# First tile turned beside the weights, two places for rows of x, for queries and for the projection's tile, bias rows fetched one block later, scatter counted in batches

## The chip, the cores and the metric

The kernel runs on one core of one Trainium2 chip. The metric is the device time of one execution in microseconds (us). Beside it there is one profiled execution, from which every row below comes; its span goes from the first to the last instruction.

## What is computed

A graph transformer layer over N = 3125 nodes with D = 1024 features and 50000 edges. In short:

```python
xn = layernorm(x)
# graph attention, 4 heads of 256: softmax over the edges (src, dst) and one loop per node
xp = xn @ W;  e = leaky_relu(a_src[src] + a_dst[dst]);  alpha = softmax of e over each dst
gnn = relu(segment_sum(xp[src] * alpha, dst) + bias)
# linear attention, 16 heads of 64
Q = elu(xn @ Wq.T + bq) + 1;  K = elu(xn @ Wk.T + bk) + 1;  V = xn @ Wv.T + bv
KV = sum over nodes of K x V;  Z = Q . K.sum(0)
mix = ((Q @ KV) / (Z + 1e-6)) @ Wo.T + bo
x = x + gnn + mix
x = x + ffn(layernorm(x))     # 1024 -> 512 -> 1024, piecewise linear gelu, fixed point
```

## The kernel before

Nodes are handled in NT = 25 tiles of T = 125. A float32 product is made of three products of fp32r parts: `high` (ScalarE) writes the rounded part of an operand and `low` (VectorE) what is left of it, and `product` runs 3 x 8 matmuls of 512 columns for each half of 1024 columns; `project` does both halves, 48 matmuls. The program is a row of blocks. In each block every engine has its own list of instructions, with semaphores between them, and the next block begins when all engines have ended this one. The names used below:

- **weights of K and V** (first block of `keys_and_values`): `SplitWeights` loads 16 blocks of 128 rows into a ring of five (`raw`), TensorE turns each into one of two PSUM places, ScalarE and VectorE split it. VectorE normalises x's first tile here. Each edge's key (src * N + dst) is stored to `edge_keys`. At its end SyncE loads the bias rows `bk_row` and `bv_row`, which lie in the places of `raw`, spread over 125 partitions, and waits for them.
- **stage K** (second block): for each tile TensorE makes keys and values, turns the next tile (`turn_rows`), and sums K x V. VectorE runs `normalise` of the next tile, the bias sums, `Edges.prepare` and the sums. ScalarE `take`s the turned tile: copies it to `xT_whole`, writes its high part, and then loads `E_row`, the next 1000 edge keys spread over 125 partitions (`Edges.load`). SyncE loads x's rows and stores `xT_whole` to `xnT`. GpSimd zeroes the count matrix (50 transfers from `zeros`, each of 128 rows of 1527 words, four in flight) and then adds edges to it: `Edges.scatter` works off units of 1000 edges, each of two batches of four indirect DMAs, and every batch waits until the batch before has landed.
- **block P** (first block of `linear_attention`): the weights of the queries and the mixing matrix, and at its end the bias rows `bq_row` and `bo_row`.
- **stage Q** (second block): for each tile the projection `query`, its elu and scaling on VectorE, `turn_rows` of the scaled queries, and the projection `mix`; `finish` adds the result to x. `Edges.prepare` goes on for units 25 to 49, with `E_row` now loaded by SyncE.
- **stage V** (`graph_values`): 2 x 25 products of 24 matmuls over the tiles, first the left then the right half of the columns. In the second half, VectorE also runs 25 passes of `Nearest.step` over rows of counts, which SyncE may load when all edges are scattered.
- after them `graph_attention` and `feed_forward`, which the change does not touch.

GpSimd's share of the edges is fixed per stage: 20 units in K, 2 in P, 23 in Q and the last 5 in V. No scheduler is at work; the order on each engine is the order of the code.

Of the kernel before, what the change touches and what calls it, by code (L numbers as in the profile page):

```python
# [31 lines left out]
UNITS_K, UNITS_P, UNITS_Q = 20, 2, 23  # L32
# [5 lines left out]
ZW, ZN = 1527, 50  # L38
# [36 lines left out]
def gps_layer(nc, x, src, dst, gnn_w, att_src, att_dst, gnn_bias, wq, bq, wk, bk, wv, bv, wo, bo,  # L75
# [4 lines left out]
    counts_fill = counts.rearrange("(k p w) -> k p w", k=ZN, p=128)  # L80
# [177 lines left out]
class Edges:  # L258
# [57 lines left out]
    def scatter_unit(self, pool, counts_cells, u, slot):  # L316
# [9 lines left out]
        for c in range(CPU):  # L326
            if c and c % BATCH == 0:
                pool.wait_ge(self.scattered, u * (16 * CPU) + 16 * c)
                pool.sem_inc(self.seen, 1)
# [4 lines left out]
    def scatter(self, pool, counts_cells, first, until):  # L334
        if first == 0:
            self.scatter_unit(pool, counts_cells, 0, 0)
            first = 1
        pairs = (until - first) // 2
        with pool.Fori(0, pairs) as i:
            for k in range(2):  # L340
                self.scatter_unit(pool, counts_cells, i * 2 + (first + k), (first + k) % 2)
        if first + 2 * pairs < until:
            self.scatter_unit(pool, counts_cells, until - 1, (until - 1) % 2)
# [55 lines left out]
def keys_and_values(nc, st, a):  # L399
# [6 lines left out]
    zeros = sb("zeros", [128, ZW])  # L406

    rows = sb("rows", [T, D])
# [3 lines left out]
    x_loaded, xn_ready, stats_seen, first_link = sem("x_loaded"), sem("xn_ready"), sem("stats_seen"), sem("first_link")  # L412


    with ExitStack() as pst:
# [9 lines left out]
        rows_loaded = psem("rows_loaded")  # L425
# [3 lines left out]
        with nc.Block() as block:  # L429
            @block.sync  # L430
            def _(sp):
                for tile, e in ((src_c, a["src"]), (dst_c, a["dst"])):
                    sp.dma_start(tile[:, :, :], e.rearrange("(b c p) -> c b p", b=CB, p=CH)).then_inc(edges_loaded, 16)
                load_rows(sp, rows, a["x"][0:T, :], x_loaded)
# [28 lines left out]
            @block.scalar  # L463
            def _(act):
                weights.take_high(act, blocks)
                act.wait_ge(zeros_set, 1)

            @block.vector
            def _(dve):
                nc.vector.memset(zeros[:, :], 0.0).then_inc(zeros_set, 1)  # L470
# [4 lines left out]
                dve.wait_ge(x_loaded, 32)  # L475
                normalise(nc, chain, rows[:, :], rows[:, :], stats, moments, root, stats_seen).then_inc(xn_ready, 1)
                dve.wait_ge(keys_turned, 1)
                nc.vector.tensor_copy(edges.keys[:, :].rearrange("p (b c) -> p b c", b=CB), ktr[0:CH, :, 0:CR]).then_inc(keys_copied, 1)
                weights.take_low(dve, blocks)
# [1193 lines left out]
```

## Time and profile before

| | |
|---|---|
| median of 3 runs | 3458.6 us (3450.61 to 3459.63) |
| the profiled execution's own time | 3460.86 us |
| its span | 3459.1 us |
| TensorE busy | 3192.6 us (92%) |
| VectorE busy | 2705.0 us (78%) |
| GpSimd busy | 1015.0 us (29%), all but its last small transfers before 1510 us |
| mean granted TensorE clock | 0.972 of full speed |

The stages in the profiled execution, by the first instructions of each block: weights of K and V to 51.4 us, K to 721.4, P to 775.7, Q to 1383.1, V to about 1705. A row of the timeline gives the start in us, the duration in us, the engine, the line, what is done, and in brackets the idle time of that engine just before it and what ended it. "SPq" and "ACTq" are DMA issues; such a row's duration is that of the issue alone.

### The profile page before, as it was taken

How to read it: one execution, taken by the hardware profiler on the slowest of the kernel's cores; microseconds unless marked ns; L12 is line 12 of the kernel's file. 1: busy time of each engine (PE TensorE's matmuls, PEld its weight loads, DVE VectorE, ACT ScalarE, POOL GpSimd, SP SyncE). 2: the span in 40 equal slices, each digit the busy share in tenths (PEclk: the TensorE clock that was granted, in tenths of full speed). 3: DMA queues.
4: the chain of work that ended last, by engine and by line, in shares of the span. 5: the costliest groups of instructions: out<-in, count | busy, mean ns of one | idle time of the engine just before them, and what ended most of it. 6: DMA issues, size and time to landing. Idle time of an engine off the chain costs nothing. (4 is left out here: it accounts for less than half of the span.)

```text
span 3459.1 us, 43729 instructions
## 1 busy us (share of the span) xinstructions
PE 3192.6 (92%) x14812; PEld 2595.8 (75%) x14812; DVE 2705.0 (78%) x4736; ACT 1129.0 (33%) x1445; POOL 1015.0 (29%) x698
## 2 busy tenths in 40 slices
PE   6899999978999998998689999998999996899998
PEld 5678888857888886776568888887788885677776
DVE  5577777757777776558699999998999875788886
ACT  2011111121111111123245555555555443445444
POOL 1256777757767667720000000000000000000000
PEclk8999999999999999999899999999999998999999
DMA  7943333343444444445588878887788765222221
GB/s 260 363 81 66 54 70 55 61 125 75 95 86 91 85 95 114 94 107 154 151 211 222 228 214 219 218 218 213 213 220 218 185 165 151 69 89 71 71 89 42
DMA packets 332845, 484.90 MB, mean 140 GB/s; under 512 B 199146, under 2 KB 199246, under 8 KB 332726
## 3 DMA queue, kind: packets, MB, share of 16 engines
q1 hardware_dynamic: 142644, 401.03, 40.8%
q0 software_dynamic: 184656, 65.68, 11.0%
q10 hardware_dynamic: 5426, 16.70, 1.3%
q8 instruction: 64, 1.05, 0.1%
q14 instruction: 55, 0.45, 0.0%
HBM read 391.39 MB, written 90.80 MB: 139 GB/s over the span
## 5 line engine op out<-in xcount | busy, mean ns | idle before, releaser
L1357 PE MATMUL G_acc<-values,whole_plain 125*125 125x257 f32 x5000 | 1117.5, 385 | 82.6 <-DVE whole_plain L1317 67.4
L1357 PEld LDWEIGHTS G_acc<-values,whole_plain 125*125 125x125 f32 x5000 | 944.0, 190 | 246.2 <-DVE whole_plain L1317 80.1
L330 POOL DMA_INDIRECT counts<-E_twins_now,E_cells_now x400 | 874.3, 2186 | 378.5 <-issue 247.6
L1252 ACT ACTIVATE whole_plain<-whole_plain,G_asrc_slope 125x750 f32<-125x750 f32 (+1 forms) x400 | 375.9, 944 | 335.0 <-DVE whole_plain L1308 333.2
L1308 DVE SCALAR_TENSOR_TENSOR whole_plain<-whole_plain,G_asrc_most 125x750 f32<-125x750 f32 (+1 forms) x400 | 412.3, 1031 | 59.0 <-PE G_acc L1357 42.3
L1317 DVE SCALAR_TENSOR_TENSOR whole_plain<-whole_plain 125x750 f32<-125x750 f32 (+1 forms) x400 | 388.4, 971 | 49.6 <-ACT whole_plain L1252 49.5
L952 DVE SCALAR_TENSOR_TENSOR N_least<-xT_plain,asrc_all,N_least 125x750 f32<-125x750 bf16 (+1 forms) x336 | 340.3, 1018 | 0.0
L1226 POOL DMA_DIRECT2D gat<-xT_plain x100 | 53.4, 535 | 972.4 <-ACT xT_plain L1268 972.4
L227 PE MATMUL V_v_ps<-whole,xT_space 128*125 128x512 f32 x1200 | 293.3, 402 | 35.2 <-DVE xT_space L255 24.1
L227 PEld LDWEIGHTS V_v_ps<-whole,xT_space 128*125 128x125 f32 x1200 | 221.3, 187 | 106.9 <-DVE xT_space L255 42.5
L227 PE MATMUL Q_q_ps<-whole,xT_space 128*125 128x512 f32 x1200 | 288.2, 399 | 13.9 <-DVE xT_space L255 13.9
L227 PE MATMUL K_v_ps<-K_wv,xT_space 128*125 128x512 f32 x1200 | 293.7, 401 | 0.0
L227 PE MATMUL K_k_ps<-whole,xT_space 128*125 128x512 f32 x1200 | 288.3, 399 | 3.4 <-DVE xT_space L255 3.4
L227 PE MATMUL Q_mix_ps<-Q_mixer,xT_space 128*125 128x512 f32 x1200 | 282.0, 393 | 2.8 <-DVE xT_space L255 2.8
L227 PEld LDWEIGHTS Q_q_ps<-whole,xT_space 128*125 128x125 f32 x1200 | 222.7, 187 | 70.0 <-DVE xT_space L255 14.7
L302 DVE SCALAR_TENSOR_TENSOR E_scratch<-E_row,E_col,E_mask 125x500 bf16<-125x500 f32 x400 | 268.3, 736 | 2.3 <-DVE E_col L294 0.3
L227 PEld LDWEIGHTS K_k_ps<-whole,xT_space 128*125 128x125 f32 x1200 | 222.3, 187 | 60.5 <-DVE xT_space L255 3.8
L251 ACT ACTIVATE xT_space<-xT_whole 128x1000 fp32r<-128x1000 f32 x100 | 104.1, 1041 | 499.7 <-PE Q_q_ps L227 251.4
L227 PEld LDWEIGHTS Q_mix_ps<-Q_mixer,xT_space 128*125 128x125 f32 x1200 | 222.2, 185 | 58.6 <-DVE xT_space L255 3.1
L227 PEld LDWEIGHTS K_v_ps<-K_wv,xT_space 128*125 128x125 f32 x1200 | 224.6, 189 | 55.2
L936 ACT ACTIVATE xT_plain<-whole_plain,N_huge 125x750 bf16<-125x750 f32 (+1 forms) x175 | 164.1, 938 | 268.0 <-DMA whole_plain<-counts 224.5
L551 ACT ACTIVATE K_raw<-K_raw 125x1024 f32<-125x1024 f32 x25 | 26.5, 1059 | 571.3 <-DVE K_raw L578 571.3
(173 smaller groups left out, 3384.1 us busy)
## 6 DMA issues: line engine op xcount, KB each, us to landing
whole_plain<-counts SPq DMA_DIRECT2D x450, 328.1 KB
whole_plain<-counts SPq DMA_DIRECT2D x150, 382.8 KB
counts<-K_zeros POOLq DMA_DIRECT2D x50, 763.5 KB, 9.0
xT_whole<-xnT SPq DMA_DIRECT2D x75, 500.0 KB, 3.6
whole_plain<-counts SPq DMA_DIRECT2D x450, 38.1 KB
xnT<-xT_whole SPq DMA_DIRECT2D x25, 500.0 KB, 7.9
gat<-xT_plain POOLq DMA_DIRECT2D x100, 125.0 KB, 4.1
E_row<-edge_keys ACTq DMA_DIRECT2D x25, 488.3 KB
```

Source lines behind the costliest of these rows:

```text
L227: last = nc.tensor.matmul(out, stationary(s, b), moving(m, b), start=(n == 0), stop=(n == len(terms) - 1))
L251: return nc.scalar.activation(out, source, ACT.Copy)
L302: chain.step(nc.vector.scalar_tensor_tensor(out=self.scratch[:, c % 2, :], in0=batch, scalar=self.col[:, c:c + 1], in1=mask, op0=ALU.is_equal,
L330: nc.gpsimd.indirect_dma_start(out=counts_cells, out_offset=bass.IndirectOffsetOnAxis(ap=self.cells_now[:, slot, c:c + 1], axis=0), in_=se ...
L551: nc.scalar.activation(ex[:, :], ex[:, :], ACT.Exp).then_inc(k_exp, 1)
L936: self.nc.scalar.activation(absent[:, n % 2, 0:w], ring[:, slot, 0:w], ACT.Relu, bias=self.huge[:, :], scale=-ABSENT).then_inc(self.absent ...
L952: self.nc.vector.scalar_tensor_tensor(out=here, in0=mask, scalar=term, in1=here, op0=ALU.subtract, op1=ALU.min).then_inc(self.least_ready, 1)
L1226: pool.dma_start(a["gat_dram"][(at + t) * T:(at + t + 1) * T, h * C:(h + 1) * C], sums[:, t, 0:C]).then_inc(gat_stored, 16)
L1252: nc.scalar.activation(here, here, ACT.Exp, bias=asrc_slope[:, u % H, j:j + 1]).then_inc(exp_ready, 1)
L1308: nc.vector.scalar_tensor_tensor(out=weight[:, k % RING, 0:w], in0=rows[:, u % 2, 0, 0:w], scalar=asrc_most[:, u % H, j:j + 1], in1=rows[: ...
L1317: nc.vector.scalar_tensor_tensor(out=here, in0=here, scalar=1.0, in1=count[:, k % RING, 0:width(u)], op0=ALU.min, op1=ALU.mult).then_inc(w ...
L1357: m = nc.tensor.matmul(acc[0:T, t, 0:CW], weight[:, k % RING, t * T:(t + 1) * T], values[:, j, u % H, :], start=(j == 0), stop=(j == NT - 1))
```

## The change

Line numbers below are those of the program before; the changed program's lines lie some 15 to 25 further down.

```diff
-UNITS_K, UNITS_P, UNITS_Q = 20, 2, 23
+BATCHES_K, BATCHES_P, BATCHES_Q = 41, 3, 47
-ZW, ZN = 1527, 50
+ZW, ZN, ZR = 1527, 50, 3
...
+    def scatter_batch(self, pool, counts_cells, u, slot, batch):
+        if batch:
+            pool.wait_ge(self.scattered, u * (16 * CPU) + 16 * BATCH)
+            pool.sem_inc(self.seen, 1)
+        for c in range(batch * BATCH, (batch + 1) * BATCH):
             nc.gpsimd.indirect_dma_start(
...
# keys_and_values
-    zeros = sb("zeros", [128, ZW])
-    rows = sb("rows", [T, D])
+    zeros = sb("zeros", [128, 1, ZW // ZR])
+    rows = sb("rows", [T, 2, D])
...
             def _(sp):
-                weights.load(sp, blocks)
-                sp.wait_ge(weights.turned, len(blocks))
-                for tile, row in ((bk_row, a["bk"]), (bv_row, a["bv"])):
-                    sp.dma_start(tile[:, :], row.partition_broadcast(T)).then_inc(rows_loaded, 16)
+                weights.load(sp, range(weights.ring))
                 sp.wait_ge(keys_made, 1)
                 sp.dma_start(a["keys_dram"].rearrange("(b c p) -> c b p", b=CB, p=CH), key_c[:, :, :]).then_inc(keys_stored, 16)
-                sp.wait_ge(rows_loaded, 32)
+                weights.load(sp, range(weights.ring, len(blocks)))
+                load_rows(sp, rows[:, 1, :], rows_of(a["x"], 1), x_loaded[1])
...
             def _(act):
-                weights.take_high(act, blocks)
+                weights.take_high(act, range(EARLY))
+                take(act, 0, 0)
+                weights.take_high(act, range(EARLY, len(blocks)))
...
             def _(pe):
-                weights.turn(pe, blocks)
+                weights.turn(pe, range(EARLY))
+                pe.wait_ge(xn_ready, 1)
+                turn_rows(nc, tr, rows[:, 0, :], ident, turned)
+                weights.turn(pe, range(EARLY, len(blocks)))
...
# stage K, SyncE
+            for tile, row in ((bk_row, a["bk"]), (bv_row, a["bv"])):
+                sp.dma_start(tile[:, :], row.partition_broadcast(T)).then_inc(rows_loaded, 16)
             def body(g, n):
-                if fixed(g, 0, NT - 2):
+                if fixed(g, 0, NT - 3):
                     sp.wait_ge(turned, g + 1)
-                    load_rows(sp, rows, rows_of(a["x"], g + 1), x_loaded)
+                    load_rows(sp, rows[:, n % 2, :], rows_of(a["x"], g + 2), x_loaded[n % 2])
...
-                pool.dma_start(a["counts_fill"][n, :, :], zeros[:, :]).then_inc(zero_filled[n % FILLS_AHEAD], 16)
+                pool.dma_start(a["counts_fill"][n, :, :, :], zeros[:, :, :].to_broadcast([128, ZR, ZW // ZR])).then_inc(zero_filled[n % FILLS_AHEAD], 16)
...
# stage Q
-    q_ps, mix_ps = ps("q_ps", [128, D]), ps("mix_ps", [128, D])
+    q_ps, mix_ps = ps("q_ps", [128, 2, D]), ps("mix_ps", [128, D])
...
             edges.load(sp, a["keys_dram"], NT)
+            for tile, row in ((bq_row, a["bq"]), (bo_row, a["bo"])):
+                sp.dma_start(tile[:, :], row.partition_broadcast(T)).then_inc(rows_loaded, 16)
             load_rows(sp, xin, a["x"][0:T, :], xin_loaded)
...
-                if fixed(g, 0, NT - 3):
-                    sp.wait_ge(xT_low, g + 2)
-                    load_turned(sp, g + 2)
+                if fixed(g, 0, NT - 4):
+                    sp.wait_ge(xT_low, g + 3)
+                    load_turned(sp, g + 3)
...
# stage Q, VectorE
                 nc.vector.tensor_scalar(ex[:, :], q[:, :], 0.0, None, ALU.min).then_inc(q_low, 1)
-                if fixed(g, 0, NT - 2):
-                    dve.wait_ge(xT_high, g + 2)
-                    low(nc, xT[:, 1, :, :], xT_whole[:, :, :], xT[:, 0, :, :]).then_inc(xT_low, 1)
...
                 nc.vector.tensor_tensor(qh, qh, rz[:, :].unsqueeze(2).to_broadcast([T, MH, MD]), ALU.mult).then_inc(q_scaled, 1)
+                if fixed(g, 0, NT - 3):
+                    dve.wait_ge(xT_high, g + 3)
+                    low(nc, xT[:, 1, :, :], xT_whole[:, :, :], xT[:, 0, :, :]).then_inc(xT_low, 1)
...
# stage Q, TensorE
-            query(0)
+            query(0, 0)
+            query(1, 1)
             def body(g, n):
-                if fixed(g, 1):
-                    mix(g - 1)
                 pe.wait_ge(q_scaled, g + 1)
                 turn_rows(nc, trq, q, ident, q_turned)
-                if fixed(g, 0, NT - 2):
+                if fixed(g, 0, NT - 3):
                     pe.wait_ge(qb_ready, g + 1)
-                    query(g + 1)
+                    query(g + 2, n)
+                mix(g)
...
# stage V
+    other = sb("xT_other", [128, KB, T])
+    xT_wholes = (xT_whole, other)
...
             load_turned(1)
+            load_turned(2)
             load_terms(0)
             for q in range(WHOLE):
-                if 1 <= q < WHOLE - 1:
+                if 1 <= q < WHOLE - 2:
                     sp.wait_ge(xT_low, q)
-                    load_turned(q + 1)
+                    load_turned(q + 2)
```

The numbers of batches: before, 40 in K, 4 in P, 46 in Q and 10 in V; now 41, 3, 47 and 9. A fill of the count matrix is now 384 rows of 509 words, read three times from the same words of `zeros`, where it was 128 rows of 1527.

How the rows of the engines moved. VectorE in the first tile of stage Q (q_ps is the query's product, xT_space<-xT_whole the low part of a coming tile, xT_space<-Q_trq that of the turned queries), before:

```order
L818 TENSOR_TENSOR Q_q<-Q_q_ps,Q_raw 125x1024
L820 TENSOR_SCALAR Q_ex<-Q_q 125x1024
L255 TENSOR_TENSOR xT_space<-xT_whole,xT_space 128x1000
L826 SCALAR_TENSOR_TENSOR Q_q<-Q_q,Q_ex 125x1024
L830 TENSOR_TENSOR Q_qk<-Q_q,Q_ks_row 125x1024
L832 TENSOR_REDUCE Q_z<-Q_qk 125x16
L834 TENSOR_SCALAR Q_z<-Q_z 125x16
L836 RECIPROCAL Q_rz<-Q_z 125x16
L839 TENSOR_TENSOR Q_q<-Q_q,Q_rz 125x1024
L255 TENSOR_TENSOR xT_space<-Q_trq,xT_space 128x1000
L294 COPY E_col<-E_keys 125x8
```

The same place in the changed program:

```order
L842 TENSOR_TENSOR Q_q<-Q_q_ps,Q_raw 125x1024
L844 TENSOR_SCALAR Q_ex<-Q_q 125x1024
L847 SCALAR_TENSOR_TENSOR Q_q<-Q_q,Q_ex 125x1024
L851 TENSOR_TENSOR Q_qk<-Q_q,Q_ks_row 125x1024
L853 TENSOR_REDUCE Q_z<-Q_qk 125x16
L855 TENSOR_SCALAR Q_z<-Q_z 125x16
L857 RECIPROCAL Q_rz<-Q_z 125x16
L860 TENSOR_TENSOR Q_q<-Q_q,Q_rz 125x1024
L255 TENSOR_TENSOR xT_space<-xT_whole,xT_space 128x1000
L255 TENSOR_TENSOR xT_space<-Q_trq,xT_space 128x1000
L294 COPY E_col<-E_keys 125x8
```

The low part of a coming tile now stands behind the scaling of the queries. SyncE waits for that low part before it loads the next tile and then `E_row`.

SyncE at the end of block P and the start of stage Q, before:

```order
L642 DMA xT_whole<-xnT 128x1000
L668 DMA Q_raw<-in_L_mix_bq 125x1024
L668 DMA Q_raw<-in_L_mix_bo 125x1024
L658 UNCONDITIONAL_BRANCH
L738 UNCONDITIONAL_BRANCH
L285 DMA E_row<-edge_keys 125x1000
L168 DMA Q_raw<-in_x 112x1024
L169 DMA Q_raw<-in_x 13x1024
L642 DMA xT_whole<-xnT 128x1000 x2
```

The same place in the changed program:

```order
L661 DMA xT_whole<-xnT 128x1000
L677 UNCONDITIONAL_BRANCH
L753 UNCONDITIONAL_BRANCH
L285 DMA E_row<-edge_keys 125x1000
L757 DMA Q_raw<-in_L_mix_bq 125x1024
L757 DMA Q_raw<-in_L_mix_bo 125x1024
L168 DMA Q_raw<-in_x 112x1024
L169 DMA Q_raw<-in_x 13x1024
L661 DMA xT_whole<-xnT 128x1000 x3
```

The two bias rows moved past the end of the block (the two branches), ahead of x's rows and of the second turned tile.

TensorE in the weights of K and V (KW_tr is a turned block of weights, K_tr the turned tile of x):

```order
-L373 MATMUL KW_tr<-ident,K_raw 128x128 x128
-L429 UNCONDITIONAL_BRANCH
-L604 UNCONDITIONAL_BRANCH
+L509 UNCONDITIONAL_BRANCH
+L514 MATMUL KP_ktr<-ident,KP_key_c 125x100 x4
+L387 MATMUL KW_tr<-ident,K_raw 128x128 x32
 L242 MATMUL K_tr<-ident,K_rows 128x125 x8
+L387 MATMUL KW_tr<-ident,K_raw 128x128 x96
```

The eight transposes of the first tile stood behind the end of the block and stand now after the fourth of 16 blocks of weights.

## Rows read from the trace of the kernel before

**Rows 1.** Window: span; busy of PE, PEld, DVE, ACT, POOL; PEclk, DMA share, GB/s.
```profile
775.50:1383.00 607.50, 582.89 (x2600) 467.74 (x2600) 461.63 (x835) 86.41 (x84) 424.77 (x230) 0.98 0.43 92
```

**Rows 2.** Timeline, end of the first block and start of stage K.
```profile
39.98 1.23 DVE L255 TENSOR_TENSOR K_wv<-KW_tr,K_wv 128x1024 fp32r<-128x1024 f32 x1 [0.72 <-ACT K_wv L251]
...
51.44 1.90 PE L242 MATMUL K_tr<-ident,K_rows 125*128 125x125 f32 x8 [12.55 <-PEq L429]
...
56.74 14.12 PE L227 MATMUL K_k_ps<-whole,xT_space 128*125 128x512 f32 x48 [3.40 <-DVE xT_space L255]
```

**Rows 3.** Timeline of GpSimd: first fills, first scatter, start of P, start of V.
```profile
53.20 2.34 POOL L528 DMA_DIRECT2D counts<-K_zeros  x4 [48.87 <-issue]
...
203.44 2.12 POOL L330 DMA_INDIRECT counts<-E_twins_now,E_cells_now  x1 [1.05 <-issue]
721.50 0.19 POOL L319 COPY E_cells_now<-E_cells 125x8 uint32<-125x8 uint32 x1 [13.88 <-POOLq L505]
...
1383.06 0.28 POOL L1073 MEMSET values<- 125x100 f32 x1 [3.14 <-POOLq L737]
```

**Rows 4.** Waits of TensorE: who waited for whom, us in total, times, longest.
```profile
PE V_v_ps L227 <- DVE xT_space L255: 24.1, 24, 5.9
PE K_tr L242 <- DVE K_rows L163: 18.7, 4, 6.1
PE Q_trq L242 <- DVE Q_q L839: 8.7, 1, 8.7
```

**Rows 5.** Windows, same columns: fills, bias rows, edge keys, a stretch of Q.
```profile
65.00:75.00 10.00, 10.00 (x45) 7.96 (x44) 7.43 (x20) 1.06 (x1) 3.14 (x5) 1.00 1.02 412
44.00:49.00 5.00, 0.00 (x0) 0.00 (x0) 0.00 (x0) 0.00 (x0) 0.00 (x0) 0.50 0.32 117
49.50:50.50 1.00, 0.00 (x0) 0.00 (x0) 0.00 (x0) 0.00 (x0) 0.00 (x0) 0.50 0.27 80
...
1010.00:1011.00 1.00, 1.00 (x11) 0.91 (x10) 0.61 (x1) 0.00 (x0) 0.00 (x0) 1.00 0.00 0
```

**Rows 6.** Timeline, end of block P and start of stage Q.
```profile
765.22 1.23 DVE L255 TENSOR_TENSOR Q_mixer<-QP_mm,Q_mixer 128x1024 fp32r<-128x1024 f32 x1 [0.23 <-ACT Q_mixer L251]
...
775.70 1.04 ACT L251 ACTIVATE xT_space<-xT_whole 128x1000 fp32r<-128x1000 f32 x1 [10.52 <-PEq L658]
...
778.03 13.64 PE L227 MATMUL Q_q_ps<-whole,xT_space 128*125 128x512 f32 x48 [13.90 <-DVE xT_space L255]
```

**Rows 7.** Timeline, one tile of stage Q on VectorE, with SyncE's issue of E_row.
```profile
999.26 1.23 DVE L818 TENSOR_TENSOR Q_q<-Q_q_ps,Q_raw 125x1024 f32<-125x1024 f32 x1 [2.13 <-PE Q_q_ps L227]
...
1001.16 1.18 DVE L255 TENSOR_TENSOR xT_space<-xT_whole,xT_space 128x1000 fp32r<-128x1000 f32 x1
...
1003.15 0.27 SPq L285 DMA_DIRECT2D E_row<-edge_keys  x1
...
1006.65 1.23 DVE L839 TENSOR_TENSOR Q_q<-Q_q,Q_rz 125x1024 f32<-125x1024 f32 x1
...
1013.90 0.16 DVE L294 COPY E_col<-E_keys 125x8 f32 x1
...
1022.40 1.22 DVE L818 TENSOR_TENSOR Q_q<-Q_q_ps,Q_raw 125x1024 f32<-125x1024 f32 x1 [2.17 <-PE Q_q_ps L227]
```

**Rows 8.** Timeline of TensorE in stage V.
```profile
1405.07 63.75 PE L227 MATMUL V_v_ps<-whole,xT_space 128*125 128x512 f32 x264 [1.48 <-DVE xT_space L255]
...
1550.69 18.65 PE L227 MATMUL V_v_ps<-whole,xT_space 128*125 128x512 f32 x72 [5.89 <-DVE xT_space L255]
...
1695.87 5.82 PE L227 MATMUL V_v_ps<-whole,xT_space 128*125 128x512 f32 x24
```

**Rows 9.** Timeline: keys' product in stage K; a double pass of stage V on VectorE.
```profile
314.58 11.41 PE L227 MATMUL K_k_ps<-whole,xT_space 128*125 128x512 f32 x48
325.83 4.54 PE L227 MATMUL K_v_ps<-K_wv,xT_space 128*125 128x512 f32 x19
...
1592.34 4.25 DVE L952 SCALAR_TENSOR_TENSOR N_least<-whole_plain,asrc_all,N_least 125x875 f32<-125x875 bf16 x4
```

More of the change, by code:

```diff
@@ L325, in scatter_unit @@
         pool.sem_inc(self.seen, 1)
[L326 to L329, printed above, removed]
+        self.scatter_batch(pool, counts_cells, u, slot, 0)
+    def scatter_batch(self, pool, counts_cells, u, slot, batch):
+        nc = self.nc
+        if batch:
+            pool.wait_ge(self.scattered, u * (16 * CPU) + 16 * BATCH)
+            pool.sem_inc(self.seen, 1)
+        for c in range(batch * BATCH, (batch + 1) * BATCH):
             nc.gpsimd.indirect_dma_start(
@@ L411, in keys_and_values, with take @@
     stats, moments, root = sb("stats", [T, 2, 6]), sb("moments", [T, 2]), sb("root", [T, 5])
-    x_loaded, xn_ready, stats_seen, first_link = sem("x_loaded"), sem("xn_ready"), sem("stats_seen"), sem("first_link")
+    x_loaded, xn_ready, stats_seen, first_link = [sem(f"x_loaded{i}") for i in range(2)], sem("xn_ready"), sem("stats_seen"), sem("first_link")
+    turned, xT_copied, xT_high, xT_low, rows_loaded = sem("turned"), sem("xT_copied"), sem("xT_high"), sem("xT_low"), sem("rows_loaded")
+    tr = ps("tr", [128, KB, 128])
+    EARLY = 4
+    def take(act, g, slot):
+        act.wait_ge(turned, g + 1)
+        nc.scalar.activation(xT_whole[:, :, :], tr[:, :, 0:T], ACT.Copy).then_inc(xT_copied, 1)
+        act.wait_ge(xT_copied, g + 1)
+        high(nc, xT[:, slot, 0, :, :], xT_whole[:, :, :]).then_inc(xT_high, 1)
     with ExitStack() as pst:
@@ L474, in _ @@
                 chain = Chain(dve, first_link)
-                dve.wait_ge(x_loaded, 32)
-                normalise(nc, chain, rows[:, :], rows[:, :], stats, moments, root, stats_seen).then_inc(xn_ready, 1)
+                dve.wait_ge(x_loaded[0], 32)
+                normalise(nc, chain, rows[:, 0, :], rows[:, 0, :], stats, moments, root, stats_seen).then_inc(xn_ready, 1)
                 dve.wait_ge(keys_turned, 1)
                 nc.vector.tensor_copy(edges.keys[:, :].rearrange("p (b c) -> p b c", b=CB), ktr[0:CH, :, 0:CR]).then_inc(keys_copied, 1)
-                weights.take_low(dve, blocks)
+                weights.take_low(dve, range(EARLY))
+                dve.wait_ge(xT_high, 1)
+                low(nc, xT[:, 0, 1, :, :], xT_whole[:, :, :], xT[:, 0, 0, :, :]).then_inc(xT_low, 1)
+                weights.take_low(dve, range(EARLY, len(blocks)))
                 dve.wait_ge(keys_copied, 1)
@@ L539, in _ @@
             edges.load(act, a["keys_dram"], 0)
-            def take(g, slot):
-                act.wait_ge(turned, g + 1)
-                nc.scalar.activation(xT_whole[:, :, :], tr[:, :, 0:T], ACT.Copy).then_inc(xT_copied, 1)
-                act.wait_ge(xT_copied, g + 1)
-                high(nc, xT[:, slot, 0, :, :], xT_whole[:, :, :]).then_inc(xT_high, 1)
-            take(0, 0)
             def body(g, n):
@@ L554, in body @@
                     act.wait_ge(xT_low, g + 1)
-                    take(g + 1, (n + 1) % 2)
+                    take(act, g + 1, (n + 1) % 2)
                     act.wait_ge(edges.cells_ready, g + 1)
@@ L605, in _ @@
         def _(pe):
-            pe.wait_ge(xn_ready, 1)
-            turn_rows(nc, tr, rows, ident, turned)
             def body(g, n):
@@ L665, in _ @@
                 load_turned(sp, 0)
-                sp.wait_ge(weights.turned, 2 * KB)
-                for tile, row in ((bq_row, a["bq"]), (bo_row, a["bo"])):
-                    sp.dma_start(tile[:, :], row.partition_broadcast(T)).then_inc(rows_loaded, 16)
-                sp.wait_ge(rows_loaded, 32)
             @block.gpsimd
             def _(pool):
-                edges.scatter(pool, a["counts_cells"], UNITS_K, UNITS_K + UNITS_P)
+                edges.scatter(pool, a["counts_cells"], BATCHES_K, BATCHES_K + BATCHES_P)
             @block.scalar
@@ L773, in _ @@
             high(nc, xT[:, 0, :, :], xT_whole[:, :, :]).then_inc(xT_high, 1)
+            act.wait_ge(q_done, 1)
+            act.wait_ge(xn_loaded, 32)
+            high(nc, xT[:, 0, :, :], xT_whole[:, :, :]).then_inc(xT_high, 1)
             def body(g, n):
[L776 to L779 removed]
                 act.wait_ge(q_low, g + 1)
                 nc.scalar.activation(ex[:, :], ex[:, :], ACT.Exp).then_inc(q_exp, 1)
[L782 removed]
+                if fixed(g, 0, NT - 3):
+                    act.wait_ge(q_done, g + 2)
+                    act.wait_ge(xn_loaded, g * 16 + 48)
+                    high(nc, xT[:, 0, :, :], xT_whole[:, :, :]).then_inc(xT_high, 1)
+                if isinstance(g, int) and g == NT - 2:
                     act.wait_ge(q_done, NT)
@@ L789, in body @@
                 high(nc, qT[:, 0, :, :], trq[:, :, 0:T]).then_inc(qT_high, 1)
-            over_tiles(act, body, **ONE)
+            over_tiles(act, body, **(ONE | dict(tail=3)))
             for b in range(KB):
```

100 lines of the change are left out of this document (53 added, 47 removed).

## The prediction

> **What bounds the kernel now.** I read the windows by stage first: TensorE works 583 of 607.5 us in Q, where VectorE with 462 and GpSimd with 425 have room [rows 1]. So its gaps are what can be won. The view of waits shows whom it waits for: in K it waits four times for x's normalised rows (18.7 us), in Q once for the scaled queries (8.7), in V 24 times for a low part (24.1, the longest 5.9) [rows 4]. Then the ends of blocks. The first block ends with TensorE idle for 12.55 us and the first projection comes at 56.74 [rows 2]; before Q it idles 13.90 us [rows 6]. The warning is in GpSimd's timeline. A block ends only when GpSimd has done its share. Its last instruction of K is over at 721.50 - 13.88 = 707.6, close to the end, and in Q it ends at 1383.06 - 3.14 = 1379.9 with a wait of only 3.1 us behind it [rows 3]: it is the last engine of Q. Whatever gives GpSimd more work there is paid for.
>
> **First block, -8 us for the block.** The bias rows are 250 rows of 4 KB, 1.02 MB; at the 117 GB/s of their window they take 8.7 us [rows 5]. VectorE's last split ends at 39.98 + 1.23 = 41.2 [rows 2]. Now nothing waits for them there. The turned first tile adds to VectorE one low part (1.2) and some waiting, say 1.6, and the barrier 0.5: the next block starts at 43.3 instead of 51.4. TensorE's first projection then needs no transposes, high or low part: about 43.5 instead of 56.74 [rows 2], 13.3 earlier. The bias rows now load under it; VectorE wants them only behind the first product, 14 us later, which covers the 8.7. The keys' store, issued earlier, is hidden by the weights. If it weren't, it would end the block as it does now, 1.6 us or so behind the bias rows.
>
> The share of 0.32 says that the bias rows use 5 of 16 engines [rows 5]. The Trainium skill ("DMA: Bandwidth & Descriptors", "Why a DMA increments its semaphore by 16 and not by 1") says that a transfer uses the largest number of engines up to 16 that divides its slowest dimension, so 125 partitions get 5, and the trace agrees. By that rule a load over 128 partitions would take 8.7 x 5/16 = 2.7 us and the edit would save 6 us less; the sum goes by the 8.7 of the row.
>
> **Stage K, +2 (-6 to +16).** TensorE alone would gain: it starts 13.3 earlier and the second place for x's rows lets them come a tile ahead, which takes most of the 18.7 us; it would end some 27 us earlier, near 690. But GpSimd doesn't follow. Its time in K is a fill phase from 53.20 to 203.44, 150 us, and 40 batches in 707.6 - 203.4 = 504, so 12.6 each [rows 3]. Now: start 8.1 earlier; one batch more, +12.6; the fills. A fill is now of rows of 2036 bytes. At 412 GB/s over 16 engines 6108 bytes take 237 ns and a third 79 ns [rows 5], if the price is by size. The edge keys' rows of 500 bytes move at 80 GB/s on 0.27 x 16 engines, 27 ns each, where size alone would make 19.4 [rows 5]: some 7 ns per row. There are 12,800 rows more, 800 per engine, so +5.6 us; the bias rows on five of the same engines give 4 more. I take +10, with ends of 0 (the fills wait for other things anyhow) and +22 (small rows lose more turns among other transfers). The last batches run without x's rows beside them, -2. GpSimd ends at 707.6 - 8.1 + 10 + 12.6 - 2 = 720, and with the 3.1 us that Q shows behind a last GpSimd the block ends at 723 instead of 721.4. So TensorE's gain of some 30 us becomes waiting at the end of K, and only what GpSimd's chain gains counts.
>
> **Block P, -8.** VectorE's last split ends at 765.22 + 1.23 = 766.45, Q starts at 775.70 [rows 6]; the bias rows stand between. Without their wait the block ends 0.5 behind the split, -8.8, and 0.8 goes to a slower clock after the longer idle time. Three batches (38 us) fit in the 45 us of this block.
>
> **Stage Q, +17 (+8 to +25).** Before, a tile takes 1022.40 - 999.26 = 23.14 us and TensorE sets it. The low part of the coming tile stands early in VectorE's row, at 1001.16, SyncE issues `E_row` at 1003.15, 0.81 behind its end, and no DMA is busy at 1010: it has landed in at most 6.85. VectorE picks it up at 1013.90 [rows 5, 7], so 4 us are spare. Now the low part comes behind the scaling of the queries, and a loop closes: low part, 0.81 to the issue, about 6.85 to the landing and 0.2 to be seen, `Edges.prepare` from 1013.90 to 1022.40 - 2.17 = 1020.23, 6.33 long, the next queries' row from 999.26 to 1006.65 + 1.23, 8.62 long, the low part 1.1: 23.9 us. Its cover is TensorE's 23.14, so it is longer by 0.75, and over 22 tiles that is +16.5. TensorE's stall would show in front of the transposes of the queries.
>
> At the ends: the first wait of 8.7 goes, because query(1) runs ahead. But the turned tile 1 now stands behind the 8.7 us of bias rows and lands about 17 us after the start, which costs 3.9 before query(1) and 1.4 behind it (13.64 long [rows 6]). At the end no query is left to run beside the last scalings, which leaves 4 us more of waiting (2.8 to 6.4). Together +0.6, so 607.4 + 17 = 624.5. GpSimd does 46 batches in 1379.9 - 775.7 = 604.2, 13.13 each; 47 take 617.3 and with the 3.1 the block would be 620.4. So even if the loop of the key row didn't bind, Q gains nothing: at least +13, less perhaps 5 if batches run faster with the DMA quieter.
>
> **Stage V, -20 (-13 to -22).** A product of 24 matmuls at full clock takes (325.83 - 314.58)/2 = 5.62 us [rows 9]. The first half takes 63.75/11 = 5.80 per tile, the second (1695.87 - 1550.69)/22 = 6.60 [rows 8]. The second `xT_whole` takes the load out of the loop: 25 x 0.18 = -4.5, and 22 x 0.98 = -21.6, less the tiles in which VectorE has a double pass: 4.25/2 = 2.1 us more [rows 9], in three tiles, so +6. That VectorE is nearly busy as long as a product without that pass makes this the upper end. The wait of 5.9, for rows of counts, stays. Sum -20.
>
> **Sum** against the profiled execution's own 3460.9 us (2.3 over the median; its span is 3459.1): K's block length: it starts 8.1 earlier and ends at 723, so +2 in all up to there; P -8; Q +17; V -20. That is 2 - 8 + 17 - 20 = -9, and 3460.9 - 9 - 2.3 = 3450.
>
> **Rivals.** *Faster, 3433.* The key row lands sooner than 6.85 us, since that is only a bound (at 6 the loop is as short as TensorE's tile), and GpSimd's batches gain from the quieter DMA: Q +8 rather than +17, and the fills come out at +3 rather than +10: K -5. Sum -5 - 8 + 8 - 20 = -25. For it: the landing is an upper bound. Against: the extra batch in K and Q is fixed. 0.22. A far case of it, in which fills gain and GpSimd isn't last in K, reaches -30 and lies in its tail.
>
> *Slower, 3472.* Fills of third-size rows cost GpSimd more: a fill then waits for its three rows' turns behind other transfers' rows. From 96 ns per row rather than 86, some 10 us go; at 105, the fill phase is +32 rather than +10: K +24, sum +13. It decides from a fill phase that is 19 us longer than I take. For it: the fills fill the DMA (share 1.02 [rows 5]), so each ns of a row's price comes out whole. Against: the 500-byte rows show only 7 ns. 0.15.
>
> *No change, about 3458.* V gains less since VectorE sets the pace there (-13), and K is at +4. Sum 0. 0.18. That the change doesn't act at all is excluded in the first block and P, whose waits fall by construction.
>
> **How the numbers follow.** Forecast 0.45, rivals as above. 0.3% is 10.4 us, about what a measurement of this kernel can tell. The forecast of -9 stands on the edge: its sizes split about four in ten faster, six in ten same. With rival one (0.22 faster), the third (0.15 of 0.18 same), and the slower one, the chances are 0.42, 0.40, 0.18. The range from 3430 to 3470 takes in -28, nearly the whole faster case, and +12, into the slower one, and leaves about 0.2 out.
>
> **What the profile after would show.** Right: the first matmuls of K at about 44; GpSimd's first scatter about 160 us behind its first fill; GpSimd last in K and in Q, its next row idle for about 3 us; TensorE idle for some 30 us at the end of K; no bias rows ahead of the end of P; in Q VectorE waiting for `E_row` in front of `E_col`, and a period near 23.9; in V low-part waits near 6 us in all but for the tiles with a double pass. Wrong: a fill phase near 150 or 185; a period of 23.1; GpSimd done well before the end of a stage; V's second half still at 6.6 per tile.

## The result and the profile after

The changed kernel takes 3512.6 us (median of 4 runs, 3506.4 to 3513.3) against 3455.1 (4 runs, 3450.6 to 3459.6): a ratio of 1.0161, 95% interval 1.0143 to 1.0179. It is 57.5 us slower, where 9 us faster was forecast, and it lies outside the range.

The stages of the profiled executions (spans 3459.1 and 3504.6 us; the one after is the fastest of its four runs), by the first instructions of the blocks, in us:

| | before | after | difference | forecast |
|---|---|---|---|---|
| first projection of K starts | 56.7 | 42.8 | -13.9 | -13.3 |
| fills: first fill to first scatter | 150.2 | 197.3 | +47.1 | +10 |
| start of P | 721.5 | 764.7 | +43.2 | +2 |
| length of P | 54.2 | 42.4 | -11.8 | -8 |
| length of Q | 607.4 | 639.5 | +32.1 | +17 |
| length of V | 322.5 | 305.0 | -17.5 | -20 |
| the rest | 1753.5 | 1753.0 | -0.5 | 0 |

The last five rows add up to the 45.5 us between the spans; the first two lie within the third. The error sits in the fills and in Q, and both had been named.

GpSimd's timeline after, in the form of [rows 3]: the first four fills, the diagonal of ones behind the last fill, the first scatter, the last indirect DMA of K; then VectorE and TensorE at the start of P, from the timeline of both.

```profile
44.27 3.18 POOL L558 DMA_DIRECT2D counts<-K_zeros  x4 [39.94 <-issue]
...
224.86 3.76 POOL L563 DMA_DIRECT2D counts<-K_ones  x1 [8.49 <-DMA counts<-K_zeros]
...
241.53 2.25 POOL L334 DMA_INDIRECT counts<-E_twins_now,E_cells_now  x1 [1.04 <-issue]
...
760.32 1.99 POOL L334 DMA_INDIRECT counts<-E_twins_now,E_cells_now  x1 [0.30 <-issue]
...
764.65 0.16 DVE L699 MEMSET QP_ones<- 125x125 f32 x1 [23.68 <-PEq L532]
764.87 3.78 PE L719 MATMUL QP_mm<-k_sum,QP_ones 125*125 125x512 f32 x4 [25.14 <-DVE QP_ones L699]
```

The diagonal in the kernel before:

```profile
187.38 3.77 POOL L533 DMA_DIRECT2D counts<-K_ones  x1 [13.06 <-issue]
```

From 44.27 to 224.86 GpSimd fills, 180.6 us where the kernel before took 134.2; the diagonal and its landing take 16.7 us behind that, and took 16.1 before. So the 47 us are in the fills themselves. 41 batches of 12.7 us follow, and 2.3 us behind the last the block ends. TensorE has been idle for 25.14 us by then. So the chain that was forecast to set K's end does set it. Only its first part was mis-sized.

The DMA view of 120 us of the fills (60 to 180) in both kernels: the queue of the fills with packets, MB and share of 16 engines, and the fills with their median time to landing. Before:

```profile
q0 software_dynamic: 7099, 38.53, 81.3%
...
counts<-K_zeros POOLq DMA_DIRECT2D x46, 763.5 KB, 8.9
```

After:

```profile
q0 software_dynamic: 4780, 25.92, 72.2%
...
counts<-K_zeros POOLq DMA_DIRECT2D x33, 763.5 KB, 14.2
```

Packets have kept their mean size (5.4 KB), as if a packet now held the three pieces of a row. What they cost has grown: 0.813 x 16 x 120 us for 38.53 MB are 24.7 bytes per ns on one engine, and now 18.7. A third of a row takes 109 ns, where the forecast had 86 and its slower rival 105.

The waits of TensorE after, over the whole kernel, in the form of [rows 4]:

```profile
PE K_tr L242 <- DVE K_rows L163: 50.7, 6, 14.7
PE QP_mm L719 <- DVE QP_ones L699: 25.1, 1, 25.1
PE Q_trq L242 <- DVE Q_q L860: 19.8, 24, 1.6
PE V_v_ps L227 <- DVE xT_space L255: 11.5, 5, 4.4
```

The wait for normalised rows has not gone with the second place for x's rows; it has grown from 18.7 to 50.7 us. The one long wait in Q (8.7) has turned into 24 short ones. That in V has fallen from 24.1 to 11.5.

One tile of Q on VectorE after, with SyncE's issue, to be read beside [rows 7]:

```profile
1103.28 1.23 DVE L842 TENSOR_TENSOR Q_q<-Q_q_ps,Q_raw 125x1024 f32<-125x1024 f32 x1 [0.32 <-issue]
...
1111.78 1.19 DVE L255 TENSOR_TENSOR xT_space<-xT_whole,xT_space 128x1000 fp32r<-128x1000 f32 x1
...
1111.92 1.07 PE L242 MATMUL Q_trq<-ident,Q_q 125*128 125x125 f32 x8 [0.87 <-DVE Q_q L860]
...
1113.76 0.27 SPq L285 DMA_DIRECT2D E_row<-edge_keys  x1
...
1121.24 0.17 DVE L294 COPY E_col<-E_keys 125x8 f32 x1 [4.77 <-DMA E_row<-edge_keys]
...
1127.50 1.22 DVE L842 TENSOR_TENSOR Q_q<-Q_q_ps,Q_raw 125x1024 f32<-125x1024 f32 x1
```

This is the loop of the prediction, piece by piece: 8.5 us from the queries' row to the low part, 1.2 for that, 0.8 to the issue, 7.5 until VectorE goes on, 6.3 of `Edges.prepare`: 24.2. TensorE waits 0.87 us for it.

### The profile page after: what moved, and what is told of

Same layout as the page of the kernel before. It is cut to its first block and busy times, and to the rows that moved or that the text cites. A ratio compares the mean times of both kernels' runs of the same rounds, so it can differ in the third digit from the quotient of the medians.

```text
span 3504.6 us, 43599 instructions
## 1 busy us (share of the span) xinstructions
PE 3203.8 (91%) x14812; PEld 2605.2 (74%) x14812; DVE 2696.6 (77%) x4736; ACT 1123.8 (32%) x1445; POOL 1017.6 (29%) x698
## 5 line engine op out<-in xcount | busy, mean ns | idle before, releaser
L227 PE MATMUL V_v_ps<-whole,xT_space 128*125 128x512 f32 x1200 | 286.7, 401 | 17.6 <-DVE xT_space L255 11.5
L227 PE MATMUL Q_q_ps<-whole,xT_space 128*125 128x512 f32 x1200 | 289.9, 401 | 12.7 <-DVE xT_space L255 11.7
L227 PEld LDWEIGHTS V_v_ps<-whole,xT_space 128*125 128x125 f32 x1200 | 225.1, 189 | 78.9 <-DVE xT_space L255 16.1
L294 DVE COPY E_col<-E_keys 125x8 f32 (+1 forms) x50 | 10.1, 202 | 270.3 <-DMA E_row<-edge_keys 270.3
## 6 DMA issues: line engine op xcount, KB each, us to landing
counts<-K_zeros POOLq DMA_DIRECT2D x50, 763.5 KB, 13.7
```

Of the source, the lines that this page charges most:

```text
L227: last = nc.tensor.matmul(out, stationary(s, b), moving(m, b), start=(n == 0), stop=(n == len(terms) - 1))
```

## The experiments

All ratios are to the kernel before, run beside them. "Phase" is from the first fill to the first scatter; in every kernel 16 to 19 us of it are the diagonal behind the fills.

**The fills' source.** `thirds_alone` puts the thirds into the kernel before, `whole_zeros` takes them out of the changed one:

```diff
-ZW, ZN = 1527, 50
+ZW, ZN, ZR = 1527, 50, 3      # thirds_alone, with the lines that use ZR
...
-ZW, ZN, ZR = 1527, 50, 3
+ZW, ZN, ZR = 1468, 52, 1      # whole_zeros
-        key_c = psb("key_c", [CR, CB, CH])
+        key_c = edges.row[0:CR, 0:CB * CH].rearrange("p (b c) -> p b c", b=CB)
```

> The kernel before with one thing of the change: the fills read a third of a row of zeros three times over. Theory (the source costs): the fills of the changed kernel take 197 us from the first to the first scatter instead of 150, because each row written is read in three pieces. Then here too: a fill phase of 190 to 200 us, GpSimd's last batch of stage K some 45 us later, and the whole some 35 to 45 us over the kernel before, about 3495. Rival (traffic): the fills are slow because x's rows come a tile earlier and the bias rows load under them. Then this kernel keeps its fill phase near 150 us and its time within 5 us of the kernel before.

> The changed kernel with fills from whole rows again: 52 fills of 128 rows of 1468 words, each read once (the edges' keys are made in the place of E_row to find the room). Source theory: the fill phase falls from 197 us to about 150, K's end comes 45 us earlier in GpSimd's chain, some 25 of them until TensorE's own chain is met, which gains too since x's rows land sooner: 40 to 47 us under the changed kernel, about 3468. Rival (traffic): the phase stays above 185 us and the time within 5 us of the changed kernel.

`thirds_alone`: phase 204.7 us, 3505.9 us, ratio 1.0136 (1.0112 to 1.0160). `whole_zeros`: phase 155.4 us, start of P at 716.1, 3464.5 us, ratio 1.0024 (1.0004 to 1.0045). The thirds cost 47 us of the 57, somewhat more than the 35 to 45 expected, and the traffic theory falls. With whole rows the change is still not faster than before: Q's loss of 34 us eats what P and V give.

**The loop of the key row.** `key_row_first` exchanges two waits of SyncE; `early_low` puts the low part back behind the minimum, and ScalarE's high part ahead of the exponential:

```diff
 # key_row_first, SyncE in stage Q
+                if fixed(g, 0, NT - 2):
+                    sp.wait_ge(edges.cells_ready, g + 1 + NT)
+                    edges.load(sp, a["keys_dram"], g + (NT + 1))
                 if fixed(g, 0, NT - 4):
                     sp.wait_ge(xT_low, g + 3)
                     load_turned(sp, g + 3)
...
-                if fixed(g, 0, NT - 2):
-                    sp.wait_ge(edges.cells_ready, g + 1 + NT)
-                    edges.load(sp, a["keys_dram"], g + (NT + 1))
...
 # early_low, VectorE in stage Q
                 nc.vector.tensor_scalar(ex[:, :], q[:, :], 0.0, None, ALU.min).then_inc(q_low, 1)
+                if fixed(g, 0, NT - 3):
+                    dve.wait_ge(xT_high, g + 3)
+                    low(nc, xT[:, 1, :, :], xT_whole[:, :, :], xT[:, 0, :, :]).then_inc(xT_low, 1)
...
-                if fixed(g, 0, NT - 3):
-                    dve.wait_ge(xT_high, g + 3)
-                    low(nc, xT[:, 1, :, :], xT_whole[:, :, :], xT[:, 0, :, :]).then_inc(xT_low, 1)
```

> The changed kernel with two waits of SyncE in stage Q exchanged: it loads E_row as soon as the last key row is used, ahead of the wait for the coming tile's low part. VectorE's list is as in the changed kernel. Theory (loop of the key row): the tile of Q takes 24.2 to 24.5 us because E_row's load starts only behind the low part; now VectorE never waits for it, the tile takes TensorE's 23.1, Q is 25 to 30 us shorter and the time about 3485. GpSimd's 47 batches then end last in Q and leave perhaps 8 of it. Rival (order on the engines): the period is long since the low part stands between the scaling and finish, or since two queries' places slow TensorE. Then the waits for E_row go, but the period stays at 24 and the time within 5 us of the changed kernel.

> The changed kernel with the high and low part of the coming tile in stage Q back in their old place, behind the minimum of the queries; all else as changed. Loop theory: E_row is issued 6.5 us earlier in the tile, VectorE no longer waits for it and TensorE's tile falls from 24.4 to 23.2 us. What is open is GpSimd: with the key row's load ahead of the low part it needed 13.7 us a batch and became the last of Q. If that load's place in the tile is what slowed it, then here it needs 13.1 as in the kernel before, 47 batches take 617 us and Q about 620 (639 in the changed kernel), the time about 3493. Rival: GpSimd is slowed by a TensorE and VectorE that move faster, whatever E_row's place; then Q is 640 or more again and the time over 3508.

`key_row_first`: VectorE's wait at `E_col` is gone, TensorE turns the queries at 1105.55 and 1128.69, 23.14 us apart as before the change, and never waits for them. So the loop was the cause of the longer tile. But the time is 3523.7 us, ratio 1.0199 (1.0182 to 1.0216), slower still, and the waits of TensorE say why:

```profile
PE V_v_ps L227 <- PEq L752: 42.4, 1, 42.4
```

It stands at the end of Q for 42.4 us until GpSimd's 47 batches are done: (1458.4 - 815.1)/47 = 13.7 us each, where the kernel before needed 13.13 and the change 13.3. `early_low` comes out between the two answers: batches of (1442.7 - 812.8)/47 = 13.4 us, Q 633 us long, the time 3508.9, ratio 1.0162 (1.0125 to 1.0198), no better than the change. GpSimd is its last engine in Q:

```profile
1445.99 0.28 POOL L1099 MEMSET values<- 125x100 f32 x1 [3.26 <-POOLq L752]
```

So behind the loop lies a second bound, GpSimd's share of batches, only 6 us away, and with the loop gone a batch takes 13.4 or 13.7 us instead of 13.3. The shorter tile alone doesn't explain that: the kernel before had it too, and a batch took 13.13 us there. Why it is 13.7 with `E_row` loaded at one place of the tile and 13.4 at another, no run here tells.

**GpSimd's share.** One batch moved from K to Q:

```diff
-BATCHES_K, BATCHES_P, BATCHES_Q = 41, 3, 47
+BATCHES_K, BATCHES_P, BATCHES_Q = 40, 3, 48
```

> The changed kernel with 40, 3 and 48 batches in K, P and Q (41, 3, 47 in the change). Theory: GpSimd ends K last, TensorE is idle for 25 us there, and in Q GpSimd has 13.9 us to spare. So K is one batch, 12 to 13 us, shorter and Q at most 3 us longer: 10 us under the changed kernel, about 3502. Rival: the batches run at the pace that the other traffic leaves them, and a batch less changes K by less than 5 us, with the whole within 4 us of the changed kernel.

The time, 3509.5 us, ratio 1.0155 (1.0138 to 1.0172), can't be told from the change. The trace can: the fill phase took 203.2 us instead of 197.3, and still P starts at 755.5 instead of 764.7. From the first scatter on, K took 508 us for 40 batches (12.65 each) against 523 for 41. So the batch costs K what was forecast, and Q, at 641.9 us, gets 2.4 longer; the phase with thirds differs by as much from profile to profile (197 to 209 us in five kernels), which can hide a batch.

**VectorE's order in K.** With whole zeros, the next tile but one is normalised ahead of `Edges.prepare` (`normalise_next` does the wait and the normalising that are taken out here, and runs once ahead of the loop):

```diff
-                if more:
-                    nxt_rows = rows[:, (n + 1) % 2, :]
-                    dve.wait_ge(x_loaded[(n + 1) % 2], g * 16 + (32 + n % 2 * 16))
-                    normalise(nc, chain, nxt_rows, nxt_rows, stats, moments, root, stats_seen).then_inc(xn_ready, 1)
...
...
                 values_of(1)
+                if fixed(g, 0, NT - 3):
+                    normalise_next(n % 2, g * 16 + (48 + (n + 1) % 2 * 16))
                 if more:
                     edges.prepare(dve, chain, g + 1)
```

> Whole rows of zeros (as whole_zeros), and in stage K VectorE normalises the tile after next ahead of Edges.prepare instead of behind it. Theory: TensorE's waits for x's normalised rows (24.7 us with whole zeros, in the fill phase) come from E_row landing late under the fills with the normalising queued behind it, not from x's rows; the second place for x's rows alone is no help, but it allows this exchange. Then those waits fall under 5 us and TensorE ends K some 20 us earlier, near 692. GpSimd's chain still ends K at about 714, so the time stays within 4 us of whole_zeros (3464). Rival: x's rows themselves land late; then TensorE's waits stay over 15 us and it ends K past 708.

In `whole_zeros` VectorE stood before the tile's normalising like this:

```profile
90.42 0.17 DVE L294 COPY E_col<-E_keys 125x8 f32 x1 [10.10 <-DMA E_row<-edge_keys]
```

In `normalise_ahead` the waits for x's rows are gone and TensorE ends K at 691.4 instead of 713.2. The rival falls: x's rows were there, but VectorE was held by the key row, which lands late under the fills. The time is 3460.6 us, ratio 1.0012 (0.9997 to 1.0026), since GpSimd ends K at 713.8 as before:

```profile
689.34 2.08 PE L644 MATMUL K_kv<-K_raw 125*64 125x64 f32 x32
716.39 3.68 PE L721 MATMUL QP_mm<-k_sum,QP_ones 125*125 125x512 f32 x4 [24.97 <-DVE QP_ones L701]
```

**All together.** `early_shares` has whole zeros, the early low part and batches 40, 3, 45; `all_mended` adds the normalising ahead with 38, 3, 45; `mended_39` is that with 39, 3, 45.

> Whole zeros, the early low part of early_low, and GpSimd's batches shared 40, 3, 45, leaving 12 to stage V. Theory: with the three troubles gone (fills' source, key row's loop, GpSimd's share) K ends when TensorE does, near 713, Q takes about 607 and V's left half hides the 12 batches (132 us of 158). First block and P keep their gains of 8 and 11, V its 20. The time is 3420 to 3428, some 1% under the kernel before. Rival (order in V): the later batches delay the rows of counts, and V gives back 10 us or more.

> As early_shares, with the normalising ahead as well and the batches shared 38, 3, 45, leaving 14 to V. Theory: TensorE's K ends near 692 and GpSimd's too (201 + 38 x 12.7 = 684), so 20 us more are won: 3402 to 3410. V's 14 batches take some 155 us and end just as its left half does; if they are late, V gives back up to 10. Rival: TensorE's waits stay in K, and the time is that of early_shares.

> As all_mended, with the batches shared 39, 3, 45, leaving 13 to V instead of 14. Theory: in all_mended GpSimd was idle for 15 us at the end of K and V's right half waited 29.5 us for its last batches, 12.4 us each. One batch moved into that idle time brings the counts 12 us earlier: V is 12 us shorter, K no longer, the time 3424 to 3430. Rival: K gets longer by what V saves (GpSimd ends it at 692 + 3), and the time stays within 4 us of 3438.

| | us | ratio | 95% interval | start of P | Q | V |
|---|---|---|---|---|---|---|
| early_shares | 3439.7 | 0.9954 | 0.9939 to 0.9969 | 712.0 | 618 | 305 |
| all_mended | 3437.8 | 0.9945 | 0.9931 to 0.9960 | 692.8 | 619 | 328 |
| mended_39 | 3427.5 | 0.9916 | 0.9893 to 0.9939 | 692.7 | 618 | 317 |

All beat both kernels, but the first two by less than expected. Q takes 618 us, not 607: inside it TensorE's waits at the head and the end of the stage add up to 31 us in `early_shares`, where they are 24 in the kernel before, and two more of its products, behind such waits, take 13.4 and 13.1 us instead of 11.3, at a granted clock of 0.84 and 0.86 of full speed. And in V a batch takes 12.4 us, so that `all_mended` gives its 20 us of K back to this wait:

```profile
PE V_v_ps L227 <- DVE xT_space L255: 36.2, 5, 29.5
```

In `mended_39`, one batch moved into GpSimd's idle 14.8 us at the end of K makes it

```profile
PE V_v_ps L227 <- DVE xT_space L255: 24.2, 5, 17.8
```

and the kernel 10 us faster, as expected. V now waits for GpSimd's last scatter, whose issue ends at 1521 us, while GpSimd is still idle for 10.5 us at the end of P and 10.8 at the end of Q. What shares cut to fit these gaps would give was not run.

**What a short piece costs.** These are the changed kernel with other numbers in one line, `ZW, ZN, ZR` (words in a row, fills, pieces of a row); `small_rows` is 509, 150, 1 with eight fills in flight, `eight_ahead` the change with `FILLS_AHEAD = 8`.

> The changed kernel with each row of a fill read as two halves (twice the same 764 words) instead of three thirds. What is asked is how the fills' price grows. With whole rows the fill phase took 150 to 159 us, with thirds 197 to 209. If each further piece of a row has its price, one piece more instead of two gives 175 to 182 us, K is some 22 us shorter than in the changed kernel and the time about 3490. Rival: reading the same words again is what costs, however often; then the phase is as with thirds, 195 or more, and the time within 5 us of the changed kernel.

> The changed kernel with 150 fills of 128 rows of 509 words, each row read once and written once (eight fills in flight, since each is a third as large). If a DMA engine pays for each 2 KB row that it reads, whatever it writes, this is as slow as the thirds: a phase of 195 to 210 us and the changed kernel's time. If the price lies in reading one short row three times for one long row that is written, then the phase is 155 to 170 us, that is by size plus some 7 ns for a row, and the time 3475 to 3485.

> The changed kernel with eight fills in flight instead of four. A fill lands 13.7 us after its issue (8.9 before) and the DMA engines' share in the phase is 0.87. Theory of the engines' own time (a packet of 6108 bytes takes longer with three reads): more in flight changes the phase by less than 8 us of 197 to 209. Rival (latency): the four in flight are too few for the longer way, and eight take the phase down to 165 to 180 us and the time by 20 us or more.

> The changed kernel with thirds of 508 words, 2032 bytes, which is a multiple of 16 where 2036 is not; 51 fills. Halves of 3056 bytes (a multiple of 16) cost nothing over whole rows, thirds of 2036 cost some 45 us. If the odd length is what costs, the phase is 155 to 165 us here. If the size does (a row below about 2 KB), it stays at 195 to 210.

> The changed kernel with thirds of 512 words, exactly 2048 bytes, 12 bytes more than in the change. By length as a multiple of 16 the phase is 155 to 165 us. By size, if the border lies just at 2048 bytes, it is so too; if the price falls slowly with size between 2036 and 3056 bytes it stays at 190 to 210.

> The changed kernel with thirds of 516 words, 2064 bytes, a little over 2048 and a multiple of 16. Border at 2048 bytes, or multiples of 16: a phase of 155 to 165 us and a time of about 3466, as with halves. Price that falls slowly with size: 190 to 210 us and about 3510.

> The changed kernel with 34 fills whose rows are three pieces of 768 words, 3072 bytes. It keeps three pieces to a row and takes the size of the halves. If the size of a piece is what matters, the phase is 155 to 170 us (the matrix is 3% larger), the time about 3468. If the third piece is what costs, it is 195 us or more.

> The changed kernel with thirds of 513 words, 2052 bytes: 4 bytes over 2048 and no multiple of 16, as 2036 is none. By the DMA queues' rows a piece of 2036 bytes costs 109 ns, pieces of 2032, 2048 and 2064 bytes 87 to 92. If a length that is no multiple of 16 is what costs, this piece takes about 109 ns and the phase 195 us or more, the time about 3510. If 2036 bytes is slow for another reason (just under 2048), it takes 88 to 92 ns, the phase is 165 to 175 us and the time about 3486.

> The changed kernel with halves of 765 words, 3060 bytes, no multiple of 16; the halves of 764 words (3056 bytes) took 126 ns a piece and a phase of 158 us. If the rest of the length over 16 costs some 20 ns with every piece, this piece takes about 146 ns and the phase is 175 to 190 us. If it costs only in short pieces, the phase is that of the halves, 155 to 162, and the time about 3467.

Time per piece is worked out from the fills' queue between 60 and 180 us as above; "by size" is the piece at the 24.7 bytes per ns of the kernel before. The figure isn't the piece's own price alone: the same 2036 bytes come out at 108 to 124 ns in seven kernels (118 in `thirds_alone`, 124 in `eight_ahead`), so that a few ns count only where the phase and the ratio say the same.

| kernel | piece, bytes | multiple of 16 | phase, us | ns per piece | by size | ratio (95%) |
|---|---|---|---|---|---|---|
| before | 6108 | no | 150.2 | 247.5 | 247 | 1 |
| whole_zeros | 5872 | yes | 155.4 | 235 | 238 | 1.0024 (1.0004 to 1.0045) |
| third_768 | 3072 | yes | 151.9 | 125 | 124 | 1.0025 (1.0014 to 1.0035) |
| half_765 | 3060 | no | 169.1 | 132 | 124 | 1.0100 (1.0084 to 1.0117) |
| halves | 3056 | yes | 158.2 | 126 | 124 | 1.0042 (1.0018 to 1.0067) |
| third_516 | 2064 | yes | 170.9 | 92 | 84 | 1.0079 (1.0063 to 1.0096) |
| third_513 | 2052 | no | 314.3 | 155 | 83 | 1.0465 (1.0447 to 1.0482) |
| third_512 | 2048 | yes | 161.8 | 87 | 83 | 1.0096 (1.0078 to 1.0114) |
| the change | 2036 | no | 197.3 | 109 | 82 | 1.0161 (1.0143 to 1.0179) |
| small_rows | 2036 | no | 211.2 | 108 | 82 | 1.0197 (1.0154 to 1.0240) |
| third_508 | 2032 | yes | 171.2 | 89 | 82 | 1.0103 (1.0084 to 1.0122) |

The queue's rows of `third_513`, of `third_512` and of `halves`, from which three of these come:

```profile
q0 software_dynamic: 4422, 16.75, 65.8%
```

```profile
q0 software_dynamic: 9202, 34.76, 76.7%
```

```profile
q0 software_dynamic: 6564, 35.64, 76.5%
```

My first theory, that each piece read for a longer row has its price, fell with `halves` (no dearer than whole rows) and `small_rows` (one read, one write, and as dear as the thirds). Latency fell with `eight_ahead`: phase 208 us, ratio 1.0188 (1.0169 to 1.0206), fills landing after 30.4 us instead of 14.2. A border at 2048 bytes fell with `third_508` against `third_516`. `third_768` clears the number of pieces. Nor does the make-up of the packets sort them: their mean size is 5.4 KB at 2032 and 2036 bytes and 3.8 KB at 2048, 2052 and 2064. What is left is a price in two parts. Pieces of about 2 KB cost 4 to 9 ns over their size, so that `third_508` and `third_516` came out between the two answers expected of them, as `half_765` did. And at three sizes a length that is no multiple of 16 bytes costs more than its neighbours: 20 ns at 2036, some 65 at 2052, 6 at 3060. `third_513` was expected at 109 ns and came at 155, so the size of this part isn't understood. At 6108 bytes it hardly shows: 24.7 bytes per ns, where the 5872 of `whole_zeros`, a multiple of 16, move at 25.0. Whether it is the length or the addresses at which the pieces then start wasn't told apart.

The Trainium skill ("DMA: Bandwidth & Descriptors", "Specifications") gives 512 bytes as the least transfer for the full rate. The runs differ: rows of 2036 bytes moved at 18.7 bytes per ns and those of 2052 at 13.3, against 24.7 for 3072, and the measurement decides.

## Why the prediction was wrong

**First block: right.** 42.8 us for the first projection (43.5 forecast), the bias rows hidden.

**Stage K: the step that failed is the price of a row of the fills.** The prediction took 7 ns over size from the edge keys' 500-byte rows, hence +5.6 us, and +10 with the bias rows. The 7 ns was a good figure for 2032 and 2064 bytes (7 and 9 ns). 2036 bytes cost 27, and the phase came out +47: with 1200 pieces for each engine, 109 ns in place of 86 are 28 of the 37 us by which it missed the forecast, and where the other 9 went was not traced. The slower rival (0.15) had the size nearly right, 105 ns, but not the reason: it had the three pieces wait for their turns behind other transfers, and three pieces to a row cost only 89 ns at 2032 bytes, 87 at 2048, and nothing over size at 3072. Its nearness is luck. The reason given against it, 7 ns over size for rows of 500 bytes, did not hold at 2036 bytes, though 500 is no multiple of 16 either. The end of the range for the fills was +22; it should have been wider, since the trace had no row of that length. Of the rest of K's sum the start (-8.9), the batch (+12.7) and the end of the block (2.3) hold; the 2 us that the last batches were to gain did not come (12.7 us each, 12.6 before).

**Also in K, hidden by GpSimd:** the forecast had TensorE done near 690 since x's rows come a tile ahead. It was done at 739.7, and at 713.2 even with whole zeros. The step "the second place takes most of the 18.7 us" took the row's releaser (normalised rows) for a late load of x; VectorE was held up one step earlier by `E_row`. `normalise_ahead` shows it.

**Block P: -11.8 for -8.** The bias rows' part is right: Q starts 0.9 us behind the last split, where it was 9.3. That the block is 3.4 us shorter up to that split wasn't tested. It is so although TensorE starts it at the lower clock, as the 0.8 of the forecast supposed: the first product takes 3.78 us at 0.50 of full speed behind 25.14 idle, and took 1.98 at full speed behind 2.06. The windows, before and after:

```profile
721.50:724.00 2.50, 1.98 (x4) 0.67 (x4) 1.74 (x4) 0.00 (x0) 1.60 (x3) 1.00 0.45 147
...
764.80:768.70 3.90, 3.83 (x6) 1.59 (x7) 1.36 (x4) 0.00 (x0) 3.00 (x2) 0.50 0.78 255
```

**Stage Q: mechanism right, size short.** The loop exists and `key_row_first` takes it away. Its landing term was 7.05 us from a window without traffic at 1010 us; it is 7.5 in the tile above, and over the stage the tile is (1404.82 - 866.50)/22 = 24.47 us instead of the forecast 23.9, so 29 us instead of 16.5. So the step that fell short is the landing of `E_row`: the prediction took what one tile of the kernel before showed for all tiles of the changed one. Why it lands later there, no run tells. The head cost 4.5 and 1.6 us of waiting (3.9 and 1.4 forecast).

**Stage V: right in the main,** -17.5 for -20, with four waits of 1.1 to 4.4 us left in the second half. To the last product it is -19.6; at the end of the block 2 us more pass than before, which wasn't looked into.

**The other rivals.** "Faster" rested on Q +8 and fills +3: neither came. GpSimd as last engine of Q, which the forecast had, did not come in the change itself (it had 13.9 us to spare), since the tile's loop was longer still; it came as soon as that was mended.

## What to carry to other kernels

A buffer made smaller to win room changes the transfer that reads it; price that transfer at its exact length, by a run if the trace has no row of it, above all where a queue is full (a share of 1.02) and its engine's chain ends a block. A second buffer helps only if what the trace calls the releaser isn't itself queued behind another wait: look one instruction further back. And where one engine's work is cut into fixed shares, a gain elsewhere can stay hidden until the shares are cut anew: here the change with whole zeros (1.0024), with the normalising ahead as well (1.0012), and with the early low part alone (1.0162, for the change's 1.0161) was in no case faster than the kernel before; together, and with batches moved to V, they gave 0.9916.

## What the hardware showed that was not expected

Rows of 2052 bytes moved at 13.3 bytes per ns on each DMA engine, rows of 2048 at 23.6: four bytes more made the fill phase 314 us instead of 162. Rows of 3072 bytes moved like those of 6108 (24.7). Twice as many fills in flight made the phase no shorter (208 us) and each fill's landing twice as late (30.4 us for 14.2). And scatter batches of four indirect DMAs took 12.4 us in V, 12.6 to 12.7 in K and 13.1 to 13.7 in Q, a difference of up to 10% in a chain of 100 batches.
